# State-space stage: next batch's projections, squares, means and gates in early-freed PSUM banks, turned products in two buffers

## What is computed

```python
proj = u @ W_in                              # z, x, B, C, dt, A, trap, angles
theta = cumsum(angles * dt)                  # an angle for each position
Bn, Cn = rmsnorm(B), rmsnorm(C)              # mean of squares, ln, exp(-0.5 .)
K = rope(Bn + B_bias, theta)                 # for each of 4 heads: "turned" keys
Q = rope(Cn + C_bias, theta)
S[i, j] = (Q_i . K_j) * decay[i, j] * step[j]     # j <= i, for each head
y = S @ x + D * x
y = y * silu(z)                              # the two "gates"
out = y @ W_out
```

## Time and profile before

| what | value |
|---|---|
| median of 3 runs | 3943.99 us (3939.72 to 3955.9) |
| the profiled execution: its own time | 3941.39 us |
| its span, first to last instruction | 3939.7 us |
| mean granted TensorE clock | 0.802 of full speed |
| busy over the span | PE 67%, DVE 61%, ACT 46%, POOL 27% |
| the state-space stage | from about 3500 to 3922 us |

### The profile page before, as it was taken

One profiled execution on the slowest core, in us unless ns is written; L12 is line 12 of the kernel. 1 busy time (PEld: TensorE's weight loads), 2 busy tenths in 40 slices (PEclk: granted clock), 3 DMA queues, 4 the chain that ended last, 5 costly groups with the idle time before them and its releaser, 6 DMA issues. The chain is left out here.

```text
span 3939.7 us, 44724 instructions
## 1 busy us (share of the span) xinstructions
PE 2622.9 (67%) x10570; PEld 1143.8 (29%) x10570; DVE 2384.4 (61%) x6077; ACT 1798.5 (46%) x3080; POOL 1067.4 (27%) x1279
## 2 busy tenths in 40 slices
PE   4544354425578747936799988867656777557776
PEld 1111343311222235622333333322221111223332
DVE  4787599973644543214556655565658999346665
ACT  3443333314665521215212217744357999635554
POOL 0123465520044307820000005500001111036664
PEclk8766555556788867867899989988878999778998
DMA  2111764222395313330211104300011111010000
GB/s 103 43 43 55 154 108 82 39 51 63 128 127 103 69 49 79 39 75 32 65 29 30 30 17 87 73 6 0 0 59 44 37 37 37 3 38 24 27 25 30
DMA packets 341772, 210.88 MB, mean 54 GB/s; under 512 B 162009, under 2 KB 327689, under 8 KB 340874
## 3 DMA queue, kind: packets, MB, share of 16 engines
q1 hardware_dynamic: 296850, 181.75, 19.2%
q0 software_dynamic: 27904, 25.46, 4.1%
q10 hardware_dynamic: 16896, 2.36, 0.4%
HBM read 136.44 MB, written 62.52 MB: 51 GB/s over the span
## 5 line engine op out<-in xcount | busy, mean ns | idle before, releaser
L2095 ACT ACTIVATE ca_pw<-ca_ps,ca_mx 128x512 f32<-128x512 f32 x512 | 345.2, 685 | 52.3 <-DVE ca_mx L2121 48.4
L2121 DVE TENSOR_REDUCE ca_mx<-ca_ps 128x1 f32<-128x512 f32 x512 | 320.2, 681 | 14.7 <-PE ca_ps L2051 12.8
L1927 DVE CUSTOM_DVE_ANT_0 mx_sums<-mx_ps,w_cst 128x512 f32<-128x512 f32 (+3 forms) x512 | 220.4, 486 | 153.6 <-PE mx_ps L1905 153.6
L2051 PE MATMUL ca_ps<-ca_qs,ca_ks 128*128 128x512 bf16 x512 | 188.4, 405 | 96.8 <-ACT ca_pw L2095 73.9
L1884 PE MATMUL gm_ps<-gm_h,w_w2f 128*128 128x512 f32 x512 | 245.4, 612 | 0.0
L1705 ACT ACTIVATE ta_pw<-ta_ps,w_cst 128x1280 f32<-128x1280 f32 x128 | 166.1, 1326 | 125.0 <-PE ta_ps L1631 119.6
L1705 ACT ACTIVATE at_pw<-at_ps 128x1280 f32<-128x1280 f32 x128 | 153.8, 1236 | 59.7 <-PE at_ps L1631 59.6
L1746 POOL MEMSET at_qs<- 128x2048 bf16 x4 | 7.0, 1805 | 639.6 <-POOLq L36 639.6
L1794 DVE TENSOR_TENSOR ta_pw<-ta_pw,w_cst 128x384 f32<-128x384 f32 x128 | 76.5, 606 | 138.5 <-ACT ta_pw L1705 137.5
L1959 ACT ACTIVATE gm_h<-gm_ps,w_w2f 128x512 f32<-128x512 f32 x64 | 44.0, 687 | 253.2 <-PE gm_ps L1884 253.2
L2040 POOL DMA_DIRECT2D GX<-ca_osb x128 | 64.7, 506 | 344.9 <-DVE ca_osb L2113 341.4
(11 more groups left out here) (555 smaller groups left out, 6900.1 us busy)
## 6 DMA issues: line engine op xcount, KB each, us to landing
Pd<-s_p SPq DMA_DIRECT2D x64, 384.0 KB, 4.0
ex_w<-e_w SPq DMA_DIRECT2D x48, 256.0 KB
ta_qs<-Pd SPq DMA_DIRECT2D x192, 64.0 KB
ta_ks<-Pd SPq DMA_DIRECT2D x192, 64.0 KB
Qd<-rp_q SPq DMA_DIRECT2D x4, 2048.0 KB, 9.6
ss_ellb<-Rd SPq DMA_DIRECT2D x32, 256.0 KB, 3.3
mx_qs<-Pd SPq DMA_DIRECT2D x192, 32.0 KB
mx_ks<-Pd SPq DMA_DIRECT2D x192, 32.0 KB
```

The costliest lines, as they stand in the source:

```text
L1927: last = v.tensor_tensor_reduce(out=sums[:, u, at:at + n], in0=ps[:, u, at:at + n], in1=cst("down")[:, T - n:T], scale=-1.0, scalar=3.0e38 ...
L2051: pe.matmul(ps[:, jk, :], ks[:, h // GH % 2, h % GH, jk * 128:(jk + 1) * 128], qs[:, h // GH % 2, h % GH, :], start=True, stop=True).then_ ...
L2095: act.activation(pw[:, h % BUF, jk, :], ps[:, jk, :], ACT.Exp, bias=mx[:, h, jk:jk + 1], accum_out=z[:, h, jk:jk + 1]).then_inc(U["exp"][j ...
L2121: v.tensor_reduce(mx[:, h, jk:jk + 1], ps[:, jk, :], AX.X, ALU.max, negate=True).then_inc(U["top"][jk], 1)
```

## The change

The diff touches only `ssm_phase`. Nothing of the arithmetic is removed except two things: the copy of the angles out of PSUM by ACT (L2448; DVE now reads bank 7 directly), and the second buffer of `th`.

- PE: the next batch's keys and queries go to banks 3 and 4, right behind `products(3)`; then both gates through bank 7; then the means, into banks 0 and 1; only then `outputs((2, 3))`, and behind it the turned projections, into banks 0 and 1. The turn-over that is left is the projection of x, the output projection, and the spread.
- ACT: both gates, squares, Ln, Exp, sines and cosines of the next batch stand behind the last decays of this one. `zs` has two buffers.
- POOL: the steps of heads 0 to 2 wait for the next batch's clamped angles (the end of `one_turn`); then `turned(0)`, `turned(1)`, weigh 0, `turned(2)`, weigh 1, `turned(3)`, the steps of head 3, weigh 2, weigh 3.
- DVE: the order stays; `t2` and `t3` have two buffers, so `prepare(h)` waits for `turned(h - 2)`.

```diff
-        zs, bc, rot, dx = sb("zs", 2, T), sb("bc", 2, T), sb("rot", 2, T), sb("dx", 256)
-        sq, xt, ang, th = sb("sq", 2, T), sb("xt", NB, 256), sb("ang", T), sb("th", 2, 3, T)
+        zs, bc, rot, dx = sb("zs", 2, 2, T), sb("bc", 2, T), sb("rot", 2, T), sb("dx", 256)
+        sq, xt, th = sb("sq", 2, T), sb("xt", NB, 256), sb("th", 3, T)
-        tb, t2, t3 = sb("tb", 2, T), sb("t2", 2, T), sb("t3", 2, T)
+        tb, t2, t3 = sb("tb", 2, T), sb("t2", 2, 2, T), sb("t3", 2, 2, T)
...
+            def keys_and_queries(i):
+                pe.wait_ge(HD["t2"][H - 1], i)
+                project(i, 3, W("in")[:, 512:640])
+                project(i, 4, W("in")[:, 640:768]).then_inc(S["bcps"], 1)
+            def means(i):
+                pe.wait_ge(HD["a"][H - 1], i)
+                pe.wait_ge(S["sq"], i + 1)
+                for n in range(2):
+                    last = pe.matmul(ps[:, n, :], cst("mean"), sq[:, n, :], start=True, stop=True)
+                last.then_inc(S["ms"], 1)
+            def turned(i):
+                pe.wait_ge(S["std"], i + 1)
+                project(i, 0, W("in_turned")[:, 0:128])
+                project(i, 1, W("in_turned")[:, 128:256]).then_inc(S["turn"], 1)
+            def gates(i):
+                pe.wait_ge(S["at"], i + 1)
+                project(i, 7, W("in")[:, 0:128]).then_inc(S["z0"], 1)
+                pe.wait_ge(S["z0sb"], i + 1)
+                project(i, 7, W("in")[:, 128:256]).then_inc(S["z1"], 1)
...
                 products(3)
                 if i + 1 < B:
+                    keys_and_queries(i + 1)
+                    gates(i + 1)
+                    means(i + 1)
+                outputs((2, 3))
+                if i + 1 < B:
                     turned(i + 1)
-                outputs((2, 3))
...
+            def gates_and_roots(i):
+                gate(i, 0)
                 act.wait_ge(S["bcps"], i + 1)
                 act.wait_ge(S["norm"], i)
+                act.activation(sq[:], ps[:, 3:5, :], ACT.Square).then_inc(S["sq"], 1)
+                gate(i, 1)
...
+                g.wait_ge(S["clamp"], i + 1)
+                steps(i, 0)
+                steps(i, 1)
+                steps(i, 2)
+                turned(i, 0)
+                turned(i, 1)
+                weighed(i, 0)
+                turned(i, 2)
+                weighed(i, 1)
+                turned(i, 3)
+                steps(i, 3)
+                weighed(i, 2)
+                weighed(i, 3)
...
                 def prepare(h):
                     v.wait_ge(HD["cps"][h], i + 1)
-                    if h:
-                        v.wait_ge(HD["turned"][h - 1], i + 1)
+                    if h >= 2:
+                        v.wait_ge(HD["turned"][h - 2], i + 1)
+                    else:
+                        v.wait_ge(HD["turned"][h + 2], i)
```

More of the change, by code:

```diff
@@ L2347, in out, with turn @@
                 last.then_inc(S["sps"], 1)
[L2349 to L2356, removed]
-                pe.wait_ge(S["yz"], i)
[L2358 to L2367, removed]
+            def turn(i):
+                pe.wait_ge(S["yz"], i)
+                pe.wait_ge(S["z1sb"], i + 1)
                 for j in range(NB):
@@ L2429, in turn @@
                 if i + 1 < B:
+                    keys_and_queries(i + 1)
[3 more added lines that the diff above has]
+                if i + 1 < B:
                     turned(i + 1)
-                outputs((2, 3))
             pe.wait_ge(S["dx"], 1)
-            project(0, 7, W("in")[:, 768:896]).then_inc(S["ang"], 1)
+            angles(0)
+            keys_and_queries(0)
+            gates(0)
+            means(0)
+            turned(0)
             for i in range(B):
-                turn(i, i == 0)
+                turn(i)
             out(B - 1)
@@ L2513, in _ @@
         def _(g):
-            for i in range(B):
[L2515 to L2546, removed]
@@ new lines, in turned, with steps @@
+            def turned(i, h):
+                g.wait_ge(HD["t2"][h], i + 1)
+                if h >= 2:
+                    g.wait_ge(HD["qk"][h - 2], i + 1)
+                else:
+                    g.wait_ge(HD["qk"][h + 2], i)
+                for n in range(2):
+                    last = g.tensor_tensor(kq[:, h % 2, K_ if n == 0 else Q_, :], t2[:, h % 2, n, :], t3[:, h % 2, n, :],
+                                           ALU.add)
+                last.then_inc(HD["turned"][h], 1)
+            def steps(i, h):
+                g.wait_ge(HD["dm"][h], i)
+                for n, c, src in ((0, 1, "stri"), (1, 2, "ident")):
+                    if n:
+                        g.wait_ge(HD["m2"][(h - 1) % H], i + 1 if h else i)
+                    last = g.tensor_tensor(mm[:, h] if n == 0 else own[:],
+                                           cst(src).unsqueeze(1).to_broadcast([128, NB, 128]),
+                                           COL[:, c, :, i * H + h:i * H + h + 1].to_broadcast([128, NB, 128]),
+                                           ALU.mult)
+                last.then_inc(HD["m1"][h], 1)
+                g.wait_ge(HD["m1"][h], i + 1)
+                g.tensor_tensor(mm[:, h], mm[:, h], own[:], ALU.add).then_inc(HD["m2"][h], 1)
@@ new lines, in weighed @@
+            def weighed(i, h):
+                g.wait_ge(HD["m2"][h], i + 1)
+                g.wait_ge(HD["dec"][h], i + 1)
+                for jk in range(NB):
+                    at = KEYS_AT[jk]
+                    d = dec[:, (i * H + h) % DB, at // T, at % T:at % T + 128]
+                    last = g.tensor_tensor(d, d, mm[:, h, jk, :], ALU.mult)
+                last.then_inc(HD["dm"][h], 1)
+            for i in range(B):
+                g.wait_ge(S["clamp"], i + 1)
[11 more added lines that the diff above has]
+                weighed(i, 3)
```

79 lines of the change are left out of this document (35 added, 44 removed).

## The result

| | before | after |
|---|---|---|
| median of the runs | 3941.85 us (3937.91 to 3955.9) | 3992.94 us (3989.49 to 3997.08) |
| profiled execution: span | 3939.7 us | 3988.4 us |
| period of a batch, mean of seven | 51.53 us | 57.23 us |
| heads (P to W), batch 2 | 31.6 us | 42.1 us |
| turn-over (W to next P), from batch 2 | 20.3 us | 14.0 us (15.4 us in the last three) |

The change makes the program slower: the ratio of the means is 1.0124, 95% interval 1.0095 to 1.0152. Forecast was 3995 us. As in the prediction, P is the start of prepare 0 in a batch and W the end of weigh 3.

A forecast was written before the change was run, and what follows sets the result against it. It took the state-space stage as bound by a chain of waits passing between engines. Seven periods (+41) and the last batch (+12.5) added 53.5 to the profiled 3941.4, giving 3995 us, range 3968 to 4016.

The forecast's parts named there:

- The ring: Heads: prepare(h + 1), turned(h + 1), weighing h, weigh h, prepare(h + 2) wait in turn; 9.8 us a head, 6.3 before.
- The steps of head 3: POOL, heads: three step instructions between turned 3 and weighing 2, costing 3.4 us on the path.
- The upward bound: PE after idling: half rate also covers the keys and gates, 2.2 us more a batch; +70, 4012 us.
- The turn-over: W to the next P: one PE queue behind weigh 2, summing to 19.6 us; shrinks from 20.4 to 14.3.
- the near tie: Before the spread: normalizing and subtraction end within half a microsecond of the output projection on PE; 0.4 us added.
- The subtraction: DVE, behind normalizing, beside PE's output projection: taken to last 0.4 us.
- The sum: Whole stage: period 57.4 against 51.5, seven times +41, last batch +12.5, first batch within 1 us; total +53.5.
- The sentence on the last batch: Last batch, no next one: W at 43.1 against 30.2, with weigh 3 of batch 7 beginning 3.6 us early; +12.5.
- The second rival: The turn-over's gain wins: heads stay at 31.5, turn-over 14.3, last batch's products +6; about 3900 us; chance 0.09.
- The lower bound: Turned at 2.5, no near tie, products(3) 2.3, shorter hand-overs: period 54.6, last batch +10, total +32, 3973 us.
- (4): Outputs((2, 3)), behind two gates and the means, delay y and all else; turn-over stays at 20; 4034 us; chance 0.05.
- (5): Half clock through the whole PE queue, from more and longer idle gaps; 4012 to 4030 us; chance 0.11.

The follow-up runs named there:

- the experiment with the keys: The changed kernel with the next batch's keys and queries moved on TensorE in front of products(3); period 54.54, one execution at 3975.91 us.
- the one with the output projection: The changed kernel with the previous batch's output projection moved on TensorE from in front of spread(0) to behind it; period 57.43, one execution at 3992.4 us.
- the first experiment: The changed kernel with GpSimd weighing head h before making turned(h + 1), and all steps in front; 3877.48 us median, ratio to before 0.9842.

## Why the prediction was right

**The ring.** It was the term that carried the forecast and it was the cause: the order of turned and weighing alone costs 8.5 us a batch in the old kernel and 51.58 - 41.96 = 9.6 in the new one. Its size was taken at 9.8 and is 9.3 (weigh 0 to weigh 1, 3642.46 to 3651.75). The 0.4 us of issue before a prepare that I carried over from the earlier trace rows isn't there when prepare's inputs have long been ready: prepare 2 starts at 3644.44, 0.2 us after weigh 0's last instruction began.

**The steps of head 3.** Costed at 3.4, measured 3.4 at weigh 2. But taking them away was worth 5.65, since the idle time that they add to TensorE brought the half clock on. I had that as a fixed 3.75 us for products(3); it was 3.83 in batch 2 and 4.61 in batch 5, where the half clock also ran on into the projections. In the last three turn-overs TensorE's queue ended 12.4 to 12.6 us after W, in the first four 11.8 to 12.1. The upward bound of the prediction had this mechanism, at 2.2 us a batch.

**The turn-over.** Predicted 14.3, measured 14.0 in the first four and 15.4 in the last three. The sum over TensorE's queue held, as the experiment with the keys shows, and the near tie was real, as the one with the output projection shows. The subtraction was mis-sized: taken at 0.4, it measured 0.44 to 1.48. The prediction asked what POOL's steps do to one_turn, by the 1.37 against 0.41 us, and not what they do to the subtraction, which now runs beside them. In the last three turn-overs the later queue made it start 11.7 to 11.9 us after W instead of 11.1 to 11.4. It then met the next step instruction, took 1.33 to 1.48 us, and TensorE idled 0.7 to 0.9 us for it: so the step from 14.0 to 15.4 is the half clock and the steps together. The sum would have been wrong as a pure queue: without the tie, moving the output projection would have paid.

**The sum.** Period 57.4 predicted, 57.23 measured; last batch +12.5 in the sum, +12.5 measured; P of batch 0 within 1 us, measured -0.8. That the period agrees to 0.2 us is luck in part. Weigh 2 was to end at P + 37.3 and ended at 36.0, since the ring is shorter; from there to the next P it was to take 20.1 us, and it took 20.1 to 22.2, 21.2 in the mean. These two cancel: -1.3 and +1.1. The sentence on the last batch gave as its reason a start of weigh 3 that no row shows. The working behind it was W at 43.1 against 30.2, which is 12.9; the number was rounded down, and W was then 42.8. The two misses cancel. The second rival's +6 for the last batch's products has no row behind it; without it, 6.1 us on seven periods and 0.9 on eight are 50, which gives 3891. The lower bound is a little too high in its own terms: turned, tie and products(3) take 1.05 + 0.4 + 1.45 = 2.9 us off 57.4, which is 54.5 before any hand-over. And 3616.73, where Exp is said to start, is the start of normalizing; Exp's row is not shown. The 3.1 us to the last Sin fit all the same: in the changed kernel it ended 3.2 us after Exp.

**The rivals.** (2), the gain of the turn-over wins, is what the first experiment built: with turned(h + 1) off the path in front of the weighing the program takes 3877, even less than that rival's 3900, since the heads take 28.8 us and not 31.5. Weigh 3 starts 6.3 us after weigh 2 there, and 7.6 before, where the decays of head 3 stood behind ACT's copy of the angles; that the copy is the reason is argued from this order, as no run took it out alone. (4), outputs too late, is out: the turn-over did shrink. (5), half clock through the whole queue, came true only for its front part: products(3) and, most in three batches, the projections right behind it. The means, outputs and turned projections behind them ran at clock 1.00 in batch 2 and took the same times in the others.

**What was to be seen.** The weighs were to start at about 12, 22, 35 and 41 us: 12.0, 21.3, 33.9, 40.0. The wait for weighed decays was to be two or three times its old size; it is 3.8 times as large. POOL was to stop waiting mainly for t2; that was wrong. It waits 124.9 us for it instead of 89.6. The statement contradicted the ring itself: in a ring both sides wait.

**The pages.** What the Trainium skill, SBUF — State Buffer, says in its part on the two physically separate sides agrees with the rows again: one_turn's second instruction took 0.43 us with POOL idle and 1.15 beside a step, and the first VectorE instruction of the stage (two SBUF inputs) 0.42 against 1.32. What the Trainium skill, TensorE: Matmul & The Clock Gate, says in its part on the clock gate agrees in direction: behind 1.7 us of idle time products(3) took 2.40 us at clock 1.00, behind 6.9 us it took 4.61 at 0.50.

## What to carry to other kernels

When two in-order engines hand work back and forth, write down for each block what the block in front of it waits for. A block moved one place forward for overlap (turned(h + 1) ahead of weighing h) turns two independent chains into one ring, and the second buffer that was to allow the overlap helps little (about 1 us a batch here), since the other engine's order still ties prepare to the weigh before. When two engines slow each other, look at what else on the path a moved block will meet: here the held steps met the subtraction. And judge an order by trying its parts: here another order of POOL's blocks turned a 1.2% loss into a 1.6% gain.

## What the runs showed of the hardware

- The same idle time of TensorE does not always bring the same clock. Outputs behind 3.19 us of idle took 4.53 us in batch 2 of the kernel before and 2.37 in batch 3; the windows view gives granted clocks of 0.50 and 1.00 for the two bursts:

```profile
3655.90:3660.40 4.50, 4.46 (x16) 1.91 (x17) 4.40 (x4) 0.00 (x0) 4.42 (x4) 0.50 0.00 0
3708.10:3710.50 2.40, 2.33 (x17) 1.29 (x17) 2.33 (x3) 0.00 (x0) 2.40 (x2) 1.00 0.04 11
```

- So a price for a burst behind idle time is a range, here 2.4 to 4.6 us, and a shortened wait can be paid back by a slower burst.
- The wait of a VectorE instruction for a GpSimd one can stand in the trace as a long instruction and not as idle time: the subtraction L2613 took 0.41 to 0.42 us with GpSimd idle and up to 1.48 beside a step. A chain that runs beside such work can move in steps of one GpSimd instruction, here from 14.0 to 15.4 us.
- Work that computes nothing can pay: six repeated projections in an idle gap made a batch 2.6 us shorter.
